# A top-4 expert layer whose tile results are stored per token and choice and summed at the end

## The reference, cut to what matters

```python
# layer 0: a subject matrix per batch row, then 8 experts, top 2, added to x
x = x + _L0_ffn_ref(_L0_cond_ref(x, itok, L0_cond_weights), Wr, Wg, Wu, Wd)

# layer 1, conditioning: SwiGLU of width 1024 with low-rank adapters per batch row
gate = _lora_linear(x, Wg, Ag, Bg, idx); up = _lora_linear(x, Wu, Au, Bu, idx)
h = _lora_linear(jax.nn.silu(gate) * up, Wd, Ad, Bd, idx)

# layer 1, expert part: 16 experts, 4 per token, and a gated shared expert of width 704
probs = jax.nn.softmax(h @ router_w.T)
top_vals, top_idx = jax.lax.top_k(probs, 4)
top_vals = top_vals / jnp.maximum(top_vals.sum(-1, keepdims=True), 1e-09)
comb = zeros((N, 16)).at[arange(N)[:, None], top_idx].add(top_vals)
y = einsum('eni,eih->enh', silu(g) * u, w_down)        # g, u: h by each expert's weights
routed = einsum('enh,ne->nh', y, comb)
shared = silu(h @ sh_gate) * (h @ sh_up) @ sh_down
x = x + routed + sigmoid(h @ sh_gate_w) * shared
```

## Time and profile before

| | |
|---|---|
| Median of 3 runs | 463.68 us (461.99 to 464.67) |
| The profiled execution's own time | 463.59 us |
| Its span | 461.5 us |
| Busy: TensorE, VectorE, ScalarE, GpSimd | 88%, 49%, 33%, 45% of the span |
| Chain that ended last | PE 54%, issue 12%, POOL 10%, DMA 10%, DVE 9% |
| DMA moved | 43.21 MB, 94 GB/s mean |

### The profile page before, as it was taken

The page is one execution under the profiler, slowest core; times in us unless marked ns, Lnnn a source line. Parts: engine busy times, 40 slices in busy tenths (PEclk is TensorE's granted clock), DMA queues, the critical chain, the costliest instruction groups (busy, mean ns, idle before and its releaser), DMA issues.

```text
span 461.5 us, 6633 instructions
## 1 busy us (share of the span) xinstructions
PE 406.7 (88%) x1884; PEld 319.5 (69%) x1885; DVE 228.0 (49%) x487; ACT 151.6 (33%) x346; POOL 206.1 (45%) x161
## 2 busy tenths in 40 slices
PE   3999999999899999999998799899998888888810
PEld 2977888887688888888786587588865655655600
DVE  6946454456821222212559999556543434434500
ACT  2525334344433323332564443232222222222100
POOL 6411313122122222221035464728887887888770
PEclk9799999999999999999999899789999999999975
DMA  7403452444533322201011453544445454445404
GB/s 223 159 5 83 127 152 83 134 157 163 204 114 115 114 96 83 85 14 55 2 34 36 131 118 113 120 149 79 66 78 77 71 87 60 77 71 68 53 1 91
DMA packets 20865, 43.21 MB, mean 94 GB/s; under 512 B 5214, under 2 KB 11774, under 8 KB 20286
## 3 DMA queue, kind: packets, MB, share of 16 engines
q1 hardware_dynamic: 11677, 31.55, 22.0%
q0 software_dynamic: 9168, 11.42, 15.4%
HBM read 35.57 MB, written 10.39 MB: 100 GB/s over the span
## 4 chain that ended last, share of the span: by engine, by line
PE 54%; issue 12%; POOL 10%; DMA 10%; DVE 9%; ACT 1%; POOLq 0%; SPq 0%; DVEq 0%; ACTq 0%
PE gu L1046 11%; PE gu L1048 10%; PE gu L1047 10%; PE y L1046 4%; PE y L1047 4%; PE y L1048 4%; DMA out<-w_raw,put 4%; DMA sg_tok<-sgT 3%; POOL out L495 2%; POOL y_b L495 2%; PE y L1316 2%; PE gu L1072 2%; PE gu L1299 2%; POOL w_hi L485 2%; POOL w_lo L485 2%
## 5 line engine op out<-in xcount | busy, mean ns | idle before, releaser
L457 POOL TENSOR_TENSOR w_lo<-w_raw,w_hi 128x512 fp32r<-128x512 f32 (+3 forms) x50 | 60.2, 1225 | 187.1 <-ACT w_hi L529 177.6
L1046 PE MATMUL gu<-act_hi,w_hi 128*128 128x512 f32 x196 | 79.0, 403 | 4.2 <-DVE hid L763 3.9
L1047 PE MATMUL gu<-act_lo,w_hi 128*128 128x512 f32 x196 | 78.0, 398 | 0.0
L1048 PE MATMUL gu<-act_hi,w_lo 128*128 128x512 f32 x196 | 77.7, 396 | 0.0
L553 ACT ACTIVATE hid_hi<-hid 128x512 fp32r<-128x512 f32 (+1 forms) x50 | 31.5, 633 | 100.9 <-DVE hid L763 60.6
L1011 DVE TENSOR_SCALAR w_raw<-y,slot_w 128x256 f32<-128x256 f32 x47 | 22.6, 481 | 61.5 <-DMA out<-w_raw,put 27.9
L1316 PE MATMUL y<-w_dn,t_hidT 88*128 x188 | 51.3, 396 | 0.6 <-DVE t_hidT L1018 0.6
L763 DVE TENSOR_TENSOR hid<-silu,gu 128x512 f32<-128x512 f32 (+1 forms) x28 | 19.2, 686 | 65.9 <-PE gu L1048 61.1
L776 DVE TENSOR_TENSOR hid_lo<-hid,hid_hi 128x512 fp32r<-128x512 f32 (+1 forms) x50 | 36.9, 740 | 29.8 <-ACT hid_hi L553 29.3
L1046 PEld LDWEIGHTS gu<-act_hi,w_hi 128*128 128x128 f32 x196 | 37.7, 193 | 13.9 <-issue 5.7
L668 ACT ACTIVATE silu<-gu 128x176 f32<-128x176 f32 x47 | 14.9, 318 | 91.4 <-PE gu L1301 91.4
(11 more groups left out here) (189 smaller groups left out, 680.0 us busy)
## 6 DMA issues: line engine op xcount, KB each, us to landing
w_raw<-in_wc SPq DMA_DIRECT2D x8, 576.0 KB, 3.7
w_raw<-in_w SPq DMA_DIRECT2D x11, 384.0 KB, 3.3
w_raw<-in_w_gu SPq DMA_DIRECT2D x8, 352.0 KB, 4.1
w_gu<-in_w_gu SPq DMA_DIRECT2D x8, 352.0 KB, 4.5
w_raw<-in_ws SPq DMA_DIRECT2D x6, 384.0 KB, 3.2
w_raw<-scr SPq DMA_DIRECT2D x8, 256.0 KB, 4.4
w_dn<-in_w_dn SPq DMA_DIRECT2D x1, 1760.0 KB
w_dn<-in_x_tok SPq DMA_DIRECT2D x2, 512.0 KB, 5.3
```

The costliest lines, as they stand in the source:

```text
L457: nc.gpsimd.tensor_tensor(w_lo[par][:, w], w_raw[par][:, w], w_hi[par][:, w].bitcast(F32), ALU.subtract).then_inc(split, 1)
L1046: T.matmul(out, w[0], x[0], start=start, stop=False)
L1047: T.matmul(out, w[0], x[1], start=False, stop=False)
L1048: return T.matmul(out, w[1], x[0], start=False, stop=stop)
```

## The change

- `slot` values shrink from three numbers to one, 4 x token + choice + 1. `get` is that less one, shifted right by two; `put` is the number less one, or for an empty slot a row in a dump area behind the 4096 rows. `slot_w`, `weight_hi` and `values` are gone, and the one-hot is 48 columns wide per token tile instead of 144.
- Tile results are copied without a weight and scattered to `y_k`, a tensor with a row for each token and choice and 512 dump rows, without addition and without bounds check. No scatter waits for another; `output` waits for scatter i-4 as before.
- After the last scatter SyncE reads `y_k` in eight pieces of 128 tokens (`y_in`, in the space of the expert weights), VectorE multiplies each of the four choices by its weight and adds it to `base`, and SyncE writes each piece of `out`. The zero fill, the early writes of `base` and the adding transfer at the end go away.
- `w1_high` and `w1_low` are called in conditioning, one piece per chunk. What lay in `w1_hi` then (adapter outputs and small weights) lies in the space of the down weights. The conditioning loops of SyncE, ScalarE and GpSimd are written out.
- SyncE issues the last shared chunk ahead of the down weights, and the down weights come in two pieces (13 and 3 experts) instead of three (10, 2 and 4).

```diff
-VALUES = 3
-ROUTE_N = VALUES * SLOT_COLS
+ROUTE_N = SLOT_COLS
...
         @block.sync
...
             raw(SH, C0[SH] + 4, C0[SH] % 2)
             sp.wait_ge(s_x2c, 4)
             sp.dma_start(d["x2"].rearrange("(t p) h -> p t h", p=P), x_tok[:]).then_inc(s_x2, 16)
+            raw(SH, C0[SH] + 5, (C0[SH] + 5) % 2)
             sp.wait_ge(s_bd, 2)
...
-            for c in range(C0[SH] + 5, C0[SH] + NC[SH]):
-                raw(SH, c, c % 2)
-            sp.wait_ge(s_slot, K1 - 1)
+            sp.wait_ge(s_slot, K1)
             w1_dn_piece(1)
-            sp.wait_ge(s_slot, K1)
-            for j in range(2):
-                sp.wait_ge(t_in[j], 16)
-            w1_dn_piece(2)
-            out_tok = d["out"].rearrange("(t p) h -> p t h", p=P)
-            for s in range(2):
-                t = slice(s * NT // 2, (s + 1) * NT // 2)
-                sp.wait_ge(s_bc, KH * (s + 1))
-                sp.dma_start(out_tok[:, t], base[:, t]).then_inc(s_base, 16)
-            sp.wait_ge(s_out, 16)
+            for j in range(RING):
+                sp.wait_ge(s_y[j], 16 * len(range(j, SLOT_TILES, RING)))
+            for t in range(NT):
+                sp.dma_start(y_in[t], d["y_k"][t * P * K1:(t + 1) * P * K1].rearrange("(p k) h -> p k h", k=K1)
+                             ).then_inc(s_fin[t], 16)
+            for t in range(NT):
+                sp.wait_ge(s_fadd[t], K1)
+                sp.dma_start(d["out"][t * P:(t + 1) * P], base[:, t]).then_inc(s_out, 16)
+            sp.wait_ge(s_out, 16 * NT)
...
         @block.gpsimd
...
-            for k in range(NC[SH]):
+            for k in range(NC[COND]):
+                low(COND, C0[COND] + k, (C0[COND] + k) % 2)
+                if k:
+                    w1_low(k - 1)
+            low(SH, C0[SH], C0[SH] % 2)
+            w1_low(NC[COND] - 1)
+            for k in range(1, NC[SH]):
                 low(SH, C0[SH] + k, (C0[SH] + k) % 2)
-                for q in (2 * k - 3, 2 * k - 2):
-                    if 0 <= q < W1_SPLITS:
-                        w1_low(q)
...
             def scatter(i, j):
-                par = j % 2
-                if i >= 2:
-                    pool.wait_ge(s_acc[par], 8 * (i - par))
-                elif i == 1:
-                    pool.wait_ge(s_base, 32)
                 pool.wait_ge(t_put, i + 1)
-                nc.gpsimd.indirect_dma_start((d["y_b"], d["out"])[par],
-                                             bass.IndirectOffsetOnAxis(ap=put[:, i:i + 1], axis=0), t_out[j], None,
-                                             bounds_check=N - 1, oob_is_err=False, compute_op=ALU.add
-                                             ).then_inc(s_acc[par], 16)
+                nc.gpsimd.indirect_dma_start(d["y_k"], bass.IndirectOffsetOnAxis(ap=put[:, i:i + 1], axis=0), t_out[j], None
+                                             ).then_inc(s_y[j], 16)
...
         @block.vector
...
-                V.tensor_scalar(t_out[j], out_ps[j % 2], slot_w[:, tile(i)], None, ALU.mult).then_inc(t_put, 1)
+                V.tensor_copy(t_out[j], out_ps[j % 2]).then_inc(t_put, 1)
...
+            dve.wait_ge(s_bc, 2 * KH)
+            for t in range(NT):
+                dve.wait_ge(s_fin[t], 16)
+                for k in range(K1):
+                    if k:
+                        dve.wait_ge(s_fadd[t], k)
+                    V.scalar_tensor_tensor(out=base[:, t], in0=y_in[t][:, k], scalar=r_top[:, t, k:k + 1], in1=base[:, t],
+                                           op0=ALU.mult, op1=ALU.add).then_inc(s_fadd[t], 1)
```

More of the change, by code:

```diff
@@ L243, in build @@
         s_scr = sem("scratch_written")
-        s_zero, s_yb = sem("zeros_ready"), sem("y_b_zeroed")
-        s_w1, s_w1d = sem("w1_gate_up_landed"), sem("w1_down_landed")
+        s_w1 = [sem(f"w1_split_landed{k}") for k in range(W1_PIECES)]
+        s_w1g, s_w1d = sem("w1_whole_landed"), sem("w1_down_landed")
         s_w1h, s_w1l = sem("w1_hi_ready"), sem("w1_lo_ready")
@@ L259, in build @@
         t_dn, t_put = sem("tile_down"), sem("tile_out_ready")
-        s_acc = [sem("y_b_added"), sem("out_added")]
+        s_y = [sem(f"choice_rows_written{j}") for j in range(RING)]
+        s_fin, s_fadd = [sem(f"choices_landed{t}") for t in range(NT)], [sem(f"choices_added{t}") for t in range(NT)]
         s_out = sem("out_written")
@@ L410, in _ @@
                 w1_piece(k)
-            run_chunks(sp, COND, 2, NC[COND], cond_chunk)
+            for c in range(C0[COND] + 2, C0[COND] + NC[COND]):
+                cond_chunk(c, c % 2)
             raw_first(SH)
@@ L466, in _ @@
                                     ALU.subtract).then_inc(s_small, 1)
-            for st in (L0, COND):
-                run_chunks(pool, st, 2 if st == L0 else 0, NC[st], lambda c, par: low(st, c, par))
+            run_chunks(pool, L0, 2, NC[L0], lambda c, par: low(L0, c, par))
             def w1_low(q):
@@ L606, in _, with w1_high @@
                     A.activation(la_hi[:, j, half(s)], la[:, j, half(s)], ACT.Copy).then_inc(s_lah, 1)
-            chunk_of(COND)(C0[COND], C0[COND] % 2)
-            units(COND, 1)
+            def w1_high(q):
+                act.wait_ge(s_w1[q], 16)
+                w = split_cols(q)
+                A.activation(w1_hi[:, w], w1_raw[:, w], ACT.Copy).then_inc(s_w1h, 1)
+            for k in range(NC[COND]):
+                c = C0[COND] + k
+                chunk_of(COND, SH if k == NC[COND] - 1 else None)(c, c % 2)
+                w1_high(k)
             for s in range(2):
@@ L964, in _ @@
             got = slot_ps[:, 0:SLOT_TILES]
-            V.tensor_scalar(get[:], got, -1.0, 0.0, ALU.add, ALU.max).then_inc(t_get, 1)
-            V.tensor_copy(slot_w[:], slot_ps[:, SLOT_COLS:SLOT_COLS + SLOT_TILES])
-            chain(V.tensor_scalar(empty[:], got, 0.0, float(4 * N), ALU.is_equal, ALU.mult))
-            V.tensor_tensor(slot_w[:], slot_w[:], slot_ps[:, 2 * SLOT_COLS:2 * SLOT_COLS + SLOT_TILES], ALU.add)
+            chain(V.tensor_scalar(get_i[:], got, -1.0, 0.0, ALU.add, ALU.max))
+            V.tensor_scalar(get[:], get_i[:], K1.bit_length() - 1, None, ALU.arith_shift_right).then_inc(t_get, 1)
+            chain(V.scalar_tensor_tensor(out=empty[:], in0=got, scalar=0.0, in1=cst1[:, CT_DUMP:CT_DUMP + SLOT_TILES],
+                                         op0=ALU.is_equal, op1=ALU.mult))
             V.scalar_tensor_tensor(out=put[:], in0=got, scalar=-1.0, in1=empty[:], op0=ALU.add, op1=ALU.add)
```

66 lines of the change are left out of this document (24 added, 42 removed).

## The result

The changed kernel took 436.5 us (median of 4 runs, 435.9 to 443.1) against 462.8 for the kernel before beside it: ratio 0.943, 95% interval 0.939 to 0.947. Forecast were 441.5 and a range of 433 to 458. Which chip that was isn't on record; I call it the first. Kernels that differ from the changed one by a small edit took as long on two numbered chips (436.9 beside 461.8 on chip 15; 434.5 beside 461.3 on chip 2), either of which may be the first. On another, chip 8, here "the fourth", the unchanged program of the changed kernel took **475.7 us against 464.2**, slower than before (ratio 1.023, 1.019 to 1.027). Medians here are over all executions of a kernel, ratios leave out slow ones, over 1.5% above its fastest (443.1 is one, at a mean clock of 0.944 against 0.959 to 0.964).

A forecast was written before the change was run, and what follows sets the result against it. The prediction took TensorE to bound the kernel up to about 328 us, then GpSimd's scatters and gathers in the expert-tile loop. Its sum: 463.6 - 6.8 - 22.8 - 1.5 + 9.0 = 441.5 us, range 433 to 458.

The forecast's parts named there:

- Scatter 1.0 us: Expert-tile loop: GpSimd's scatter without bounds check and addition takes 1.0 us instead of 1.59, ends 0.95 and 1.64.
- Rival (a): Tile loop: the plain scatter still costs 1.59 us because direction sets it; total 468.6 us, slower by 1.1%; 14%.
- (b): Tile loop: scatter price in between, 1.1 to 1.4 us; at 1.25 the total is 453 us; 10%.
- Loop -22.8: Tiles 3 to 46: 43 steps at TensorE's 2.41 us plus 0.7 for output buffers, 104.3 instead of 127.1 us.
- Drain -1.5: Tile 46's first matmul to the last output's end: 5.8 us instead of 7.3, outputs no longer waiting for accumulations.
- Fold +9.0, 24.5 us: After the last output: last scatter, y_k reads, 32 chained additions and output write take 24.5 us where 15.5 stood.
- Rival (c): Fold: the reads of y_k crawl, 34 us instead of 18.4, total 457 us; 5%.
- Shared stage -6.8: Shared-expert stage: gaps -4.9, slow clock -1.4, narrower slot matmuls -1.0, a split meeting the adapter +0.5; ends 0 and -11.
- Conditioning +0.5: Conditioning: splits moved there are free, except the last, which meets the adapter's low part TensorE waits for: +0.5 us.
- Closing 4.2, carried over: End of the span: 4.2 us of closing behind the last landing, kept unchanged in the forecast.
- d: Main case, the forecast as summed, own range 434 to 448 us; 68%.
- e: Main case with the clock held over tiles 0 and 1 or faster additions: 433 us and less; 3%.

The follow-up runs named there:

- the second experiment: Against the changed kernel, the scatter adds into y_k again, without bounds check, y_k zero-filled first: 468.7 us.
- e8_one_addition: Against the changed kernel, three of the fold's four additions per token left out, all eight reads of y_k kept: 432.0 us.
- e7_last_out_pool: Against the changed kernel, the last of the eight output transfers issued by GpSimd instead of SyncE: 443.8 us.
- e2_add: Same run as the second experiment: accumulating scatter into zero-filled y_k, no bounds check, against the changed kernel: 468.7 us beside 461.8 for the kernel before.
- e5_piece_held: Against the changed kernel, the second piece of w1_dn (528 KB) issued only after the first two gathers landed: 434.5 us.

## Why the prediction came out as it did

On the first chip, term by term (profiled execution 436.4, forecast 441.5):

- **Scatter 1.0 us.** Right (0.99). The reason given, that both removed features are the difference, was half right: it is the accumulation. Rival (a), direction sets the price, and (b) are refuted by the changed kernel's own scatter rows; the second experiment adds why.
- **Loop -22.8.** It was -23.7, 0.2 beyond what was called the best possible, since the step is 2.40 and not 2.41. The 0.7 for the ring of four buffers wasn't needed: TensorE never waits.
- **Drain -1.5.** It was -1.6 (7.3 to 5.7).
- **Fold +9.0, 24.5 us.** It was 24.1, with errors that cancel: additions 15.8 instead of 14.7 (0.49 apart, not 0.46), the last scatter's start 0.7 behind the last output instead of 0.2, its landing 2.4 instead of 3.0, first read 3.3 instead of 3.7, last output 1.7 instead of 2.8. Rival (c), crawling reads, did not come: 1.48 us each (e8_one_addition), less than half of the 3.2 that the prediction works out for a transfer on GpSimd's path, which these are not.
- **Shared stage -6.8.** Tile 3 begins 6.4 us earlier, with errors inside that cancel. The start had lost 1.2, for which there was no term. The stage up to `get` gained 9.3 where 7.3 were forecast (4.9, 1.4 and 1.0), although the 32 slot matmuls at a third of the columns gave next to nothing. The first gather I forecast at about 282, and it started at 280.91. The step that failed is that the gap before its turn "stays": it was 3.55 us instead of 2.13, as the gather took 6.3 us to land instead of 3.0, and the turn came at 287.25. I had named the last piece travelling with it and put no price on it; held back, the turn is 2.6 us sooner. The gate's transfer took 18.0 us as forecast (17.6), but ended at 278.9 and not 277, so the spread gate, at 283.3, was no longer "hidden": it travelled beside the gather too. The low clock behind the wait, which the -6.8 had left in, came again, for 6.8 us (10.2 before).
- **Conditioning +0.5.** It was +0.2 (TensorE is 1.2 us behind the kernel before when it starts and 1.4 when it ends).
- **Closing 4.2, carried over.** The most mis-sized term: it measured 0.4, and 3.8 of the 5.1 us of error are there. I had taken a stretch at the end of a span as a constant, without asking which engine it belonged to. e7_last_out_pool brings it back.
- **Outside the span** 2.1 was 1.8.
- **Chances.** Those of d, e, b and c add up to 0.86, so "faster" with a little of a should be more than the 0.84 stated.

On that chip the mechanism was the forecast one; that the total lies within 5 us owes a little to errors that cancel in the fold and in the shared stage.

What the prediction had no term for is a loop whose steps are 38% longer on one chip. All of its 13% for slower stood on the scatter's price; 475.7 lies outside the range, and none of the rivals is its cause.

## What to carry to other kernels

Price a software scatter by its operation: accumulation cost 0.60 us of GpSimd a time here, a bounds check 0.03, and writing to separate rows and adding once at the end was cheaper by 16.7 us than 47 accumulating, bounds-checked scatters (loop -23.7, drain -1.6, end +8.6) where TensorE could use the time. Ask of every stretch in a span, the closing too, whose it is: in these kernels GpSimd's last instruction had to stand 8 us or more ahead of the end to cost nothing. Where small transfers decide when TensorE restarts, hold the large ones back until they have landed; and measure a loop that has no slack left on more than one chip before calling it a gain.

## What the runs showed of the hardware

- GpSimd's closing drain ended 7.8 us behind its last instruction in all traces with a plain scatter, transfer or addition there (for instance 411.7 to 419.5, 432.9 to 440.7, 463.0 to 470.8). Behind accumulating ones it was otherwise: 6.0 us behind the scatter of e2_add (444.5 to 450.5), 10.9 behind the 1024 KB transfer of the kernel before (450.4 to 461.3), 3.8 and 3.9 us after the landing.
- Eight slot products with 48 columns take 0.97 us, with 144 columns they took 1.01.
- How long TensorE waited for the first gather didn't tell what clock followed. Waits of 2.13 and 3.55 us were followed by 0.50 (1.2 GHz) for 7 us or more, and 0.95 and 1.05 us by 1.00 (2.4 GHz); but on the fourth chip 2.27 us by 1.00 and 1.07 us by 0.70 and then 0.50. A part of what e5_piece_held shows may be that.
- GpSimd's additions of 128x256 (0.84 each) made VectorE's beside them 0.66 instead of 0.50, though two engines shared the work.
